# A four-layer graph network on one core: the gate stage with three groups in flight, and the edge stage's turned one-hots made by ScalarE

## The reference, cut to what matters

```python
h = relu(layernorm(x))
x = x + L0(h)          # attention over edges, then a gate; its end:
    agg  = segment_sum(v[src] * sa, dst);  skip = feat @ Ws + bs
    g    = sigmoid(concat([skip, agg, skip - agg]) @ Wg + bg)
    rst  = g * skip + (1 - g) * agg
    rst  = (rst - mean) * rsqrt(var + 1e-5) * gamma + beta
    rst  = where(rst >= 0, rst, alpha * rst)
h = relu(layernorm(x))
x = x + L1(h)          # its start:
    e    = concat([h[row], h[col]]) @ mlp_w1 + mlp_b1
    ew   = sigmoid(gelu(e) @ mlp_w2 + mlp_b2)     # one weight per edge
    deg  = segment_sum(ew, col) + 1;  dinv = rsqrt(deg)
    xt   = h @ conv_w      # scaled and summed over edges by later stages
```

## Time and profile before

| what | value |
|---|---|
| median of 3 runs | 6144.79 us (6141.55 to 6146.19) |
| profiled execution, its own time | 6146.72 us |
| its span in the trace | 6144.7 us |
| busy: TensorE, VectorE, ScalarE, GpSimd | 4523.9, 3671.7, 3653.4, 4148.7 us |
| gate stage, in the trace | about 1193.6 to 1391.6 us |
| edge stage, in the trace | about 1391.6 to 2494.8 us |

### The profile page before, as it was taken

How to read it: one execution, slowest core, us unless ns; L and a number is a source line. 1 busy time by engine, 2 the same in 40 slices (tenths; PEclk the granted TensorE clock), 3 DMA queues, 4 the chain that set the end, 5 groups by cost and what they waited for, 6 DMA issues and landing times. The chain is left out here.

```text
span 6144.7 us, 106723 instructions
## 1 busy us (share of the span) xinstructions
PE 4523.9 (74%) x30944; PEld 3483.7 (57%) x30944; DVE 3671.7 (60%) x13296; ACT 3653.4 (59%) x7549; POOL 4148.7 (68%) x4218
## 2 busy tenths in 40 slices
PE   5666666547777777787799999699999945555555
PEld 3665666536666666677555555555555544444544
DVE  5777777764444444898544444354444446676665
ACT  3888888643333333798544444444444458888885
POOL 2777777427777777654577777477777737777773
PEclk9888888755666666899899999899999965555556
DMA  4444444205555555675222222122222223333332
GB/s 139 132 134 133 134 134 133 63 27 143 153 154 152 151 152 153 188 223 157 56 58 60 58 60 58 53 57 59 59 60 58 57 61 82 82 82 84 82 83 56
DMA packets 406933, 617.70 MB, mean 101 GB/s; under 512 B 82126, under 2 KB 260130, under 8 KB 406386
## 3 DMA queue, kind: packets, MB, share of 16 engines
q0 software_dynamic: 154368, 345.37, 21.5%
q1 hardware_dynamic: 248754, 264.52, 15.4%
q10 hardware_dynamic: 3264, 0.99, 0.1%
HBM read 530.85 MB, written 79.70 MB: 99 GB/s over the span
## 5 line engine op out<-in xcount | busy, mean ns | idle before, releaser
L1203 POOL DMA_INDIRECT sum_rows<-tab_row,src_idx x1496 | 1448.5, 968 | 604.3 <-issue 453.2
L1269 PE MATMUL sum_pX<-sum_mask,sum_part 128*128 128x512 bf16 x6174 | 1399.1, 381 | 0.0
L1230 ACT ACTIVATE sum_hot<-iota,local 128x128 f32<-128x128 f32 x1664 | 530.7, 389 | 873.4 <-PE sum_pA L1298 865.5
L1351 DVE TENSOR_TENSOR acc<-acc,sum_pA 128x128 f32 x1664 | 474.3, 285 | 958.7 <-PE sum_pA L1298 932.4
L634 POOL DMA_INDIRECT l_rows<-tab_qv,src_idx x832 | 791.5, 951 | 358.6 <-issue 248.3
L373 POOL DMA_INDIRECT l_rows<-tab_ax,src_idx x832 | 834.5, 1003 | 277.1 <-issue 253.2
L634 POOL DMA_INDIRECT l_rows<-tab_wh,src_idx x832 | 785.7, 944 | 345.0 <-issue 252.3
L1269 PEld LDWEIGHTS sum_pX<-sum_mask,sum_part 128*128 128x128 bf16 x6174 | 607.3, 98 | 655.9 <-issue 10.0
L677 PE MATMUL l_pA<-l_hotA,l_wrow 128*128 128x128 f32 x3328 | 653.5, 359 | 100.0 <-ACT l_hotA L723 47.6
L719 ACT ACTIVATE l_hotA<-iota,local 128x128 f32<-128x128 f32 x1664 | 525.8, 386 | 200.5 <-PE l_pA L677 200.5
L677 PEld LDWEIGHTS l_pA<-l_hotA,l_wrow 128*128 128x128 f32 x3328 | 577.8, 262 | 118.4 <-ACT l_hotA L723 107.1
(11 more groups left out here) (302 smaller groups left out, 8986.8 us busy)
## 6 DMA issues: line engine op xcount, KB each, us to landing
l_line<-dst_at SPq DMA_DIRECT2D x312, 256.0 KB, 3.5
spill<-l_rows SPq DMA_DIRECT2D x104, 512.0 KB
sum_rows<-spill SPq DMA_DIRECT2D x104, 512.0 KB
sum_line<-src_lo SPq DMA_DIRECT2D x104, 256.0 KB
sum_rows<-tab_row,src_idx POOLq DMA_INDIRECT x1496
l_rows<-tab_qv,src_idx POOLq DMA_INDIRECT x832
l_rows<-tab_ax,src_idx POOLq DMA_INDIRECT x832
l_rows<-tab_wh,src_idx POOLq DMA_INDIRECT x832
```

The lines of the kernel that those rows point to most:

```text
L1203: nc.gpsimd.indirect_dma_start(rows[:, g % R, u, :], None, tab_row, bass.IndirectOffsetOnAxis(src_idx[:, t:t + 1], 0)).then_inc(s_rows[g % ...
L1230: last = nc.scalar.activation(hot[:, q % HOTS, u, :], iota[:], ACT.Square, scale=-1.0, bias=local[:, t:t + 1])
L1269: last = nc.tensor.matmul(pX[:, k % 2, :], part[:, i, h, :], mask[:, step % MASKS, :], start=h == 0 and i == 0, stop=h == NB - 1 and i == 2)
```

## The change

**Edge stage.** `turned_onehots` leaves VectorE. ScalarE makes the squares of batch n+2 right after the gelu of batch n (`turned_squares`, two operations of 1024 columns) and the Relu of 1 minus them after the sigmoid of batch n (one of 2048 columns). Those of batches 0 and 1 are made before the loop.

**Gate stage.** `node_phase("gate")` is replaced by `gate_phase`, with the same computation. In round i VectorE mixes group i first, then evicts group i-2, then joins group i-1. ScalarE's round is gate i, evict i-2, first norm i, second norm i-1, turned copies i-1. The temporaries have two buffers. VectorE evicts only the 64 columns that need a bias; ScalarE copies the other 192, 128 to `keep` and 64 to `slab`, without the zero bias, and the store becomes two DMAs per group, one from `slab` and one from `keep`. Transposes wait for each block of the norm by itself, the first copy of four blocks starts after four transposes, and the first four matmuls wait for that copy alone. Square roots use the same table load as before.

The diff, cut to its core:

```diff
...
                     def _(act_e):
+                        def turned_squares(n):
+
+                            of = line[:, n % LB, :]
+                            act_e.wait_ge(s_line[n % LB], 16 * (n // LB + 1))
+                            if n >= 2:
+                                act_e.wait_ge(s_dst, n - 1)
+                            nc.scalar.activation(hotT[:, n % 2, 0, :], of, ACT.Square, bias=minus_p[:]).then_inc(s_squareT, 1)
+                            nc.scalar.activation(hotT[:, n % 2, 1, :], of, ACT.Square, bias=minus_q[:]).then_inc(s_squareT, 1)
+
+                        def turned_onehots(n):
+
+                            act_e.wait_ge(s_squareT, 2 * n + 2)
+                            nc.scalar.activation(hotT[:, n % 2], hotT[:, n % 2], ACT.Relu, scale=-1.0, bias=one[:]
+                                                 ).then_inc(s_hotT, 1)
+
                         nc.scalar.activation(part[:, 0, :], near["b"][:], ACT.Copy).then_inc(s_part, 1)
                         act_e.wait_ge(s_part, 2)
                         nc.scalar.activation(part[:, 1, :], left, ACT.Copy).then_inc(s_part, 1)
+                        for n in range(2):
+                            turned_squares(n)
+                            turned_onehots(n)
                         for n in range(BATCHES):
                             b = n % 2
                             act_e.wait_ge(s_pre, n + 1)
                             if n >= 2:
                                 act_e.wait_ge(s_logit, n - 1)
                             nc.scalar.activation(act[:, b], pre[:, b], ACT.Gelu).then_inc(s_act, 1)
+                            if n + 2 < BATCHES:
+                                turned_squares(n + 2)
                             act_e.wait_ge(s_logit, n + 1)
                             nc.scalar.activation(score[:, n * TB:(n + 1) * TB], logit[:, b], ACT.Sigmoid,
                                                  bias=col[:, 0:1]).then_inc(s_edge, 1)
+                            if n + 2 < BATCHES:
+                                turned_onehots(n + 2)
                         act_e.wait_ge(s_dend, 2)
                         nc.scalar.activation(dinv[:], dinv[:], ACT.Sqrt).then_inc(s_sqrt, 1)
 
                     @block.vector
                     def _(dve):
-                        def turned_onehots(n):
-
-                            b = n % 2
-                            dve.wait_ge(s_line[n % LB], 16 * (n // LB + 1))
-                            if n >= 2:
-                                dve.wait_ge(s_dst, n - 1)
-                            nc.vector.tensor_scalar(hotT[:, b, 0, :], line[:, n % LB, :], minus_p[:], 0.0,
-                                                    ALU.add, ALU.is_equal)
-                            nc.vector.tensor_scalar(hotT[:, b, 1, :], line[:, n % LB, :], minus_q[:], 0.0,
-                                                    ALU.add, ALU.is_equal).then_inc(s_hotT, 1)
-
...
-                        turned_onehots(0)
-                        turned_onehots(1)
...
                         for n in range(BATCHES):
-                            if n + 2 < BATCHES:
-                                turned_onehots(n + 2)
                             mlp_out(n)
...
+        def gate_phase():
...
+                    @block.sync
+                    def _(sp):
+                        for g in range(GROUPS):
+                            sp.wait_ge(s_eva, (g + 1) * GB)
+                            sp.dma_start(rows_of(tab_ax, g, 0, HF), slab[:, g % 2]).then_inc(s_st[g % 2], 16)
+                            sp.dma_start(rows_of(tab_ax, g, HF, HF + F), of_group(keep, g)).then_inc(s_st[g % 2], 16)
...
+                        def project(g):
+
+                            if g >= 1:
+                                pe.wait_ge(s_hT, 2 * g)
+                            for u in range(GB):
+                                pe.wait_ge(s_h, g * GB + u + 1)
+                                nc.tensor.transpose(pH[:, u, :], hb[:, g % 2, u, :], ident[:]).then_inc(s_ht, 1)
+                            for u in range(GB):
+                                n = g * GB + u
+                                if u == 0:
+                                    pe.wait_ge(s_hT, 2 * g + 1)
+                                if u == FIRST:
+                                    pe.wait_ge(s_hT, 2 * g + 2)
+                                if n >= RING:
+                                    pe.wait_ge(s_eva, n - RING + 1)
+                                nc.tensor.matmul(pG[:, n % RING, 0:2 * F], hT[:, u * P:(u + 1) * P], w_of["gate"][:],
+                                                 start=True, stop=True).then_inc(s_mm, 1)
+
+                        turn_sums(0)
+                        for i in range(GROUPS + 1):
+                            if i + 1 < GROUPS:
+                                turn_sums(i + 1)
+                            if i >= 1:
+                                project(i - 1)
...
+                        def evict(g):
+
+                            if g >= 2:
+                                ae.wait_ge(s_st[g % 2], 32 * (g // 2))
+                            for u in range(GB):
+                                n = g * GB + u
+                                p = pG[:, n % RING, :]
+                                ae.wait_ge(s_evd, n + 1)
+                                nc.scalar.activation(keep[:, n, :], p[:, HF:HF + F], ACT.Copy)
+                                nc.scalar.activation(slab[:, g % 2, u, :], p[:, 0:HF], ACT.Copy).then_inc(s_eva, 1)
+
+                        for i in range(GROUPS + 2):
+                            if i < GROUPS:
+                                gate(i)
+                                deviation(i, 0, s_var1, s_std1)
+                            if i >= 2:
+                                evict(i - 2)
+                            if i < GROUPS:
+                                mixed_norm(i)
+                            if 1 <= i <= GROUPS:
+                                deviation(i - 1, 1, s_var, s_std)
+                                normalise(i - 1)
+                                turned(i - 1)
...
+                        def evict(g):
+
+                            for u in range(GB):
+                                n = g * GB + u
+                                dve.wait_ge(s_mm, n + 1)
+                                nc.vector.tensor_tensor(near["b"][:, n * HF:(n + 1) * HF],
+                                                        pG[:, n % RING, HF + F:2 * F], b_gate[:, HF + F:2 * F], ALU.add
+                                                        ).then_inc(s_evd, 1)
+
+                        nc.vector.memset(near["b"][:, NB * HF:(NB + 1) * HF], 0.0)
+                        for i in range(GROUPS + 2):
+                            if i < GROUPS:
+                                gate_input(i)
+                                mix(i)
+                            if i >= 2:
+                                evict(i - 2)
+                            if i < GROUPS:
+                                scale_shift(0, i, s_std1, s_nb1)
+                            if 1 <= i <= GROUPS:
+                                join(i - 1)
+                                scale_shift(1, i - 1, s_std, s_nb)
...
-        node_phase("gate")
+        gate_phase()
```

159 lines of the change are left out of this document (added).

## The result

| | before | after |
|---|---|---|
| median of the runs | 6144.03 us | 6092.14 us |
| runs | 6141.55 to 6146.19 | 6089.19 to 6093.4 |
| span of the profiled execution | 6144.7 us | 6091.6 us |
| gate stage, start to the edge stage's first gather | 1193.6 to 1392.2 | 1193.2 to 1353.7 |
| edge stage, first gather to last | 1086.8 us | 1071.2 us |

The ratio is 0.9915, with a 95% interval of 0.9898 to 0.9932: 52 us faster, against 53 predicted. The first gather starts 38.5 us earlier, of which 0.5 us was won ahead of the stage: 38 for the gate stage (37 predicted). From the first gather to the last it is 15.6 us less (17 predicted). The other stages gave back 1 us.

What follows compares the result with a forecast made beforehand. GpSimd's gather chain bounds the edge stage; a chain around the engines, none full, bounds the gate stage. 6146.7 - 37 (gate) - 17 (edge) = 6092.7 us, the median 1.9 lower: 6091, range 6060 to 6118.

Steps and rivals of the forecast that it cites:

- What bounds the edge stage: Edge stage: it lasts as long as GpSimd's chain of 832 gathers plus 0.30 us between each two.
- Norm to mixing: Gate stage: block-by-block transposes and an earlier first copy shorten this part from 7.35 to about 5.5 us per period.
- Evictions: Gate stage: ScalarE evicts first and takes VectorE's 192-wide half, so evictions fall from 6.56 to 3.4 us per period.
- Join: Gate stage: the join's first operation, 2.45 us, gets clear of GpSimd's skip product and falls to 0.68; gain 1.8 us.
- The train of affine operations: Gate stage: GpSimd's 14 affine operations delay the previous group's join by 1.1 us per period, bounds 0 and 5.6.
- The 1 us for the two stores: Gate stage: splitting each store into two DMAs, one with 256-byte rows, costs 0 to 2 us more, taken as 1.
- Edge stage: Gathers: removing VectorE's one-hots shortens long ones from 1.38 to 1.25 us, L483's delay remaining; 17 us gained, between 12 and 41.
- ScalarE: Edge stage: two squares and a Relu add at most 4.6 us per batch; nobody waits, so the cost is 0.
- Rival A: Edge stage: L483 holds no gather, so the stage gains everything, 41 us; total 6067 us; chance 0.18.
- Rival B: Gate stage: GpSimd's affine train starves the join, period 25 us, gate gain only 10; total 6118 us; chance 0.11.
- Rival C: Edge stage: another two-SBUF-input operation, above all L461, lies at gathers' starts; no edge gain, total 6108 us; chance 0.10.
- Rival D: Edge stage: TensorE takes over at 10.9 us per batch against 10.4, 52 us slower; total 6160 us; chance 0.04.

Runs made afterwards that it cites:

- experiment 1: Kernel after, with ScalarE also writing the sigmoid to PSUM and VectorE's multiplication L495 reading it there: ratio to before 0.9876.
- experiment 5: Kernel after without the gate stage's affine part (times gamma, plus beta), GpSimd's 14 operations per group becoming one on a single column: 6098 us beside 6149 for before.
- experiments 3 and 4: Each half of the change alone on the kernel before: first the new gate stage, ratio 0.9933; then the one-hots on ScalarE, ratio 0.9978.
- experiment 2: Kernel before, one-hots still on VectorE, with the multiplication L483 reading the sigmoid from PSUM instead of SBUF: ratio 1.0001.
- experiment 8: Kernel after, with one-hots back on VectorE behind their batch's product and reduction, and the multiplication's sigmoid in PSUM: 6075 us, one run.

## Why the prediction was right, point by point

- **What bounds the edge stage.** Right. GpSimd waits only for issue in every run, and every gain there was read first in the sum of its gathers: 32.5 - 7.6 = 25 us less in experiment 1, 24 us in the time.
- **Norm to mixing**, 5.5: 5.58. Undone, the period grew by 1.90.
- **Evictions**, 3.4: 3.87. Block 4 is multiplied 0.79 us after the first eviction, as reckoned, but the step from there left out the time from the start of a matmul to its own eviction, 1.23 us (1252.42 to 1253.65), part of which the spacing does not cover.
- **Join**: -1.8 right (2.45 to 0.68). The train of affine operations, 1.1: 0.65, by experiment 5 0.62. L1965 lost 0.29 and L1966 0.14, not 0.4 each, and two small operations behind them 0.2. GpSimd's first products lost more: two took 1.71 instead of 0.87. The two misses of a half us cancelled, so the period was 20.47 for 20.5, and the stage 155.3 us (1193.17 to the last store's issue at 1348.46) for 155.7: in the total that is luck. The 1 us for the two stores was not there: from the last issue to the first gather it was 5.2 us before and 5.3 after, so the stage gained 38 and not 37.
- **Edge stage**, 17: 15.6. The step "the one-hots hold the gather up, and L483's 0.30 is hidden under them" was wrong in kind and near in number. L483 held the gather first (0.34), and the one-hots added only the 0.09 us that L445 still ran at the second place. Long gathers went from 1.38 to 1.28 us on average (32.5 us less the setup's 5.8 and some 0.3 of small ones, over 79 gathers, are 0.33 each), not to 1.25: 76 x 0.09 + 81 x 0.05 + 20 x 0.2 = 15, where the sum of the gathers fell by 15.4. How many gathers L495 would hold the prediction took over from the kernel before (76); it was 73 in after, but the scatter shown under experiments 3 and 4 says that 9 to 19 us could have come out. That it was 15.6 for 17 is in part luck.
- **ScalarE**, at most 4.6 us more: 4.25 (two squares of 1.13, a Relu of 1.99), all beside other work, as said.
- **Rival A**, no hold by L483 (6067 us): refuted by the 79 gathers that stayed long, and by experiment 1, which removed them. What made it the forecast, that such an operation and a gather don't meet, holds only at the second place in a gather. **Rival B**: refuted by experiment 5. **Rival C**, the bad position moves to the product: it did not happen in the change (6 gathers held by L473 in after), but did in experiment 2, where it took the whole gain. That it stayed away was not for the reason given alone; without one-hots the product follows 0.4 us behind the gather's start and ends before the next one.
- **Rival D**, TensorE takes over: no, but it came nearer than the chance of 0.04 says. The granted clock and busy time, edge stage (columns: stretch, its length, busy us of PE, PEld, DVE, ACT, POOL, PE clock as a share of full speed, DMA share, GB/s), of before, then of after:

```profile
1500.00:2400.00 900.00, 666.93 (x5553) 598.93 (x5551) 421.96 (x691) 301.51 (x347) 689.35 (x692) 0.63 0.57 152
```

```profile
1500.00:2400.00 900.00, 859.24 (x5615) 731.72 (x5615) 356.83 (x527) 653.71 (x614) 686.44 (x702) 0.51 0.58 154
```

The waits (us in total, times, longest), of before over the same stretch, then of after over 1500 to 2380 us:

```profile
PE l_pD L402 <- DVE l_hi L483: 229.5, 86, 4.1
...
DVE l_pre L454 <- PE l_pK L393: 72.9, 13, 5.8
```

```profile
DVE l_pre L466 <- DMA l_rows<-tab_ax,src_idx: 531.1, 86, 7.7
...
PE l_pK L391 <- ACT l_hotT L433: 28.3, 61, 0.5
PE l_pD L403 <- DVE l_hi L495: 8.3, 15, 1.0
```

TensorE now works at a mean of 0.51, so nearly all the time at 0.50, the lower level of 1.2 GHz, is 95% busy, and pauses 1.0 us at most; before it stood up to 4.1 us ahead of the degree matmuls, and by the mean of 0.63 about a quarter of the stretch was granted 2.4 GHz. VectorE waits for the rows alone, so the slower matmuls cost nothing. In experiment 1 TensorE is busy 859 of 880 us: there it is almost the bound, and a further gain on the gathers might run into it; no run tries that.

## To carry over

Where one engine issues transfers back to back, add up what each takes over its undisturbed length, and look at what the neighbour engine runs across the start of the long ones: here, with the one-hots out of the way, one operand in PSUM instead of SBUF brought 25 us, more than taking the whole one-hot work off VectorE had, and in the kernel before the same operand brought nothing. A delay that is removed shifts everything behind it, so work out which operation then stands at the sensitive place before counting a gain; an unchanged total can be one hold in place of another. And a number that comes out as expected doesn't show its reason: the gather's length in experiment 2 was right to 0.01 us, and only the rows beside it showed the cause.

## What the runs showed of the chip that was not expected

- An indirect gather has two places at which VectorE can hold it, 0.13 and 0.83 us after its start. An operation with two SBUF inputs holds it at the first only (delay: its end less 0.13 us; in after each of the 74 times that it began at least 0.03 us ahead, with one input in PSUM 0 of 84 times), the bf16 one-hots with one input at both.
- The order decides who waits: where the multiplication began less than 0.03 us ahead of the gather, the gather took 0.95 (11 of 11 in after).
- A gather gets in between two queued operations of VectorE: three passed a train of eight 0.5 us subtractions, and one left its wait at the end of the first of two one-hots.
- The granted clock of TensorE went from a mean of 0.63 to 0.51 although its own instructions did not change; what changed is that its pauses of up to 4.1 us became pauses of up to 1.0. With the one-hots back on VectorE (experiment 8) it was 0.61 over 1500 to 2380 us. Why is not settled by these runs.
- One edge stage, unchanged, took 1067.3 to 1077.7 us in six traces, by how often the multiplication began ahead of a gather.
